# All adjacency loads on SyncE's queue instead of two queues, and half of the x loads of the prologue on GpSimd's

## The reference

```python
h = jnp.maximum(_layernorm(x), 0.0)                     # x: 4096 x 256 f32
mask = (adj > 0)
agg = mask @ h / jnp.maximum(mask.sum(1), 1.0)
combined = concat([h @ W_self + b_self, agg @ W_nb + b_nb])
x = x + relu(combined @ W_comb + b_comb)
h = jnp.maximum(_layernorm(x), 0.0)
Wh = (h @ W).reshape(n, 4, 64)
sl, sr = einsum(Wh, a_l), einsum(Wh, a_r)
e = leaky_relu(sl[:, :, None] + sr.T[None], 0.2)
alpha = softmax(where(adj | eye, e, -inf), axis=2)
x = x + elu(einsum('nhm,mhd->nhd', alpha, Wh))
```

## Time and profile before

| | |
|---|---|
| median of 3 runs | 863.46 us (859.91 to 865.07) |
| the profiled execution | 861.41 us, its span 859.6 us |
| PE busy | 796.0 us, 93% |
| DVE busy | 697.7 us, 81% |
| ACT busy | 562.6 us, 65% (issuing DMAs isn't counted) |
| POOL busy | 176.4 us, 21% |
| HBM read, written | 98.17 MB, 16.85 MB |
| ACT's queue (q10), SP's queue (q1), POOL's queue (q0) | 37.89 MB, 56.32 MB, 20.86 MB |

### The profile page before, as it was taken

One profiled execution on the slowest core, in us unless ns is written; L12 is line 12 of the kernel. 1 busy time (PEld: TensorE's weight loads), 2 busy tenths in 40 slices (PEclk: granted clock), 3 DMA queues, 4 the chain that ended last, 5 costly groups with the idle time before them and its releaser, 6 DMA issues.

```text
span 859.6 us, 26116 instructions
## 1 busy us (share of the span) xinstructions
PE 796.0 (93%) x10791; PEld 728.7 (85%) x10791; DVE 697.7 (81%) x1339; ACT 562.6 (65%) x840; POOL 176.4 (21%) x254
## 2 busy tenths in 40 slices
PE   5787769999999999879999999999999999999995
PEld 4333558888888888678999999999999999999995
DVE  3777747777777777587888999889999889998884
ACT  3464112222222222489999998999989999989992
POOL 0311136577667666200000000000000000000000
PEclk9999989999999999979999999999999999999998
DMA  6599999999999999230052012401201410111001
GB/s 153 151 270 262 302 293 306 312 296 336 298 264 288 276 281 250 86 84 26 0 98 49 14 35 49 92 17 38 49 12 37 98 49 12 37 49 49 9 16 37
DMA packets 90084, 115.68 MB, mean 135 GB/s; under 512 B 61580, under 2 KB 63440, under 8 KB 90032
## 3 DMA queue, kind: packets, MB, share of 16 engines
q1 hardware_dynamic: 67680, 56.32, 25.2%
q10 hardware_dynamic: 12384, 37.89, 15.9%
q0 software_dynamic: 9968, 20.86, 8.0%
HBM read 98.17 MB, written 16.85 MB: 134 GB/s over the span
## 4 chain that ended last, share of the span: by engine, by line
PE 61%; DVE 18%; ACT 9%; issue 6%; ACTq 4%; DMA 2%; DVEq 0%
PE ps_t L573 12%; PE ps_t L575 12%; PE ps_x L635 8%; PE ps_t L635 8%; PE ps_a L635 8%; ACT stage L770 5%; DVE stage L1067 4%; ACTq L333 4%; PE ps_w L635 4%; PE ps_h L635 4%; PE ps_w L594 2%; DVE stage L1057 2%; DVE stage L1078 2%; DVE g L1093 2%; PE ps_a L542 1%
## 5 line engine op out<-in xcount | busy, mean ns | idle before, releaser
L573 PE MATMUL ps_t<-g,mask 128*128 128x257 f16 x1024 | 231.1, 275 | 3.0 <-DVE mask L965 2.9
L575 PE MATMUL ps_t<-g,mask 128*128 128x256 f16 x1024 | 231.0, 274 | 0.0
L770 ACT ACTIVATE stage<-rows,sr 128x1024 int8<-128x1024 f32 x192 | 204.3, 1169 | 5.7 <-PE ps_w L635 5.7
L770 ACT ACTIVATE stage<-bits,sr 128x1024 int8<-128x1024 f32 x192 | 204.2, 1168 | 2.5 <-PE ps_w L635 2.5
L1067 DVE SCALAR_TENSOR_TENSOR stage<-stage,mask 128x1024 int32<-128x1024 int32 x128 | 156.1, 1220 | 21.8 <-ACT stage L770 21.1
L635 PE MATMUL ps_x<-g,stage 128*128 128x130 f16 x2048 | 158.8, 220 | 9.9 <-DVE stage L1078 4.7
L635 PE MATMUL ps_t<-g,stage 128*128 128x130 f16 x2048 | 158.6, 219 | 0.0
L635 PE MATMUL ps_a<-g,stage 128*128 128x130 f16 x2048 | 158.5, 219 | 0.0
L635 PEld LDWEIGHTS ps_x<-g,stage 128*128 128x128 fp8e4 x2048 | 127.4, 97 | 12.0 <-issue 11.9
L635 PEld LDWEIGHTS ps_a<-g,stage 128*128 128x128 fp8e4 x2048 | 127.4, 97 | 0.2
L635 PEld LDWEIGHTS ps_t<-g,stage 128*128 128x128 fp8e4 x2048 | 127.2, 97 | 0.2
(11 more groups left out here) (135 smaller groups left out, 826.5 us busy)
## 6 DMA issues: line engine op xcount, KB each, us to landing
mask<-in_adj ACTq DMA_DIRECT2D x84, 256.0 KB, 12.3
mask<-in_adj SPq DMA_DIRECT2D x68, 256.0 KB, 11.2
stage<-in_adj ACTq DMA_DIRECT2D x58, 256.0 KB, 9.2
stage<-in_adj SPq DMA_DIRECT2D x46, 256.0 KB, 8.6
own_scratch<-mask POOLq DMA_DIRECT2D x16, 256.0 KB, 5.0
rows<-own_scratch POOLq DMA_DIRECT2D x32, 128.0 KB, 6.7
rows<-in_x POOLq DMA_DIRECT2D x128, 32.0 KB, 7.2
x_scratch<-late POOLq DMA_DIRECT2D x32, 128.0 KB, 8.9
```

The lines of the kernel that those rows point to most:

```text
L573: nc.tensor.matmul(ps_t32[e][:, 0:D + 1], at, g[:, 2 * kk + b, D:2 * D + 1], start=kk + b == 0, stop=kk == NK - 1 and b == 1, skip_group_c ...
L575: last = nc.tensor.matmul(ps_t32[e][:, 0:D], at, g[:, 2 * kk + b, 0:D], start=False, stop=kk == NK - 1 and b == 1, skip_group_check=True)
L770: nc.scalar.activation(sign_bytes(sgn, k, b), srow[gr % 2].rearrange("p (r n) -> p r n", n=2 * P), ACT.Sign, bias=sr[:, 2 * k + b, H + gr ...
```

## The change

ACT issues no adjacency any more. SP issues all four quarters of every piece, in the order 0, 2, 1, 3: piece 0 behind the loads of x pairs 2 and 3; pieces 1 to 6 in halves, one half behind each x pair from 4 to 15; the rest behind those. Of each x pair from 4 on SP issues two transfers (0, 2) and POOL the other two (1, 3), on a semaphore of their own, `x_half_in`, for which `variances` waits too. The table `issued_at` goes.

```diff
-        def x_rows(eng, k):
+        def x_rows(eng, k, parts, landed):
-            for a in range(UN):
-                eng.dma_start(xin[k % XR][a * UP:(a + 1) * UP, :], x_v[a, k]).then_inc(x_in[k % XR], 16)
+            for a in parts:
+                eng.dma_start(xin[k % XR][a * UP:(a + 1) * UP, :], x_v[a, k]).then_inc(landed[k % XR], 16)
...
-            x_rows(sp, 2)
-            x_rows(sp, 3)
+            x_rows(sp, 2, (0, 2, 1, 3), x_in)
+            x_rows(sp, 3, (0, 2, 1, 3), x_in)
+            adj_rows(sp, 0, (0, 2, 1, 3))
             for k in range(XR, NK):
                 sp.wait_ge(h_ready, k - XR + 1)
-                x_rows(sp, k)
-            for n in range(BOTH, 2 * NT):
-                adj_rows(sp, n, range(UN // 2))
+                x_rows(sp, k, (0, 2), x_in)
+                adj_rows(sp, k // 2 - 1, (1, 3) if k % 2 else (0, 2))
+            for n in range(NK // 2 - 1, 2 * NT):
+                adj_rows(sp, n, (0, 2, 1, 3))
...
+            def x_half(k):
+                pool.wait_ge(h_ready, k - XR + 1)
+                x_rows(pool, k, (1, 3), x_half_in)
+
+            x_half(XR)
+            x_half(XR + 1)
             for k in range(NK):
                 store_own(k)
+                if k + XR + 2 < NK:
+                    x_half(k + XR + 2)
                 if k == 2:
                     row(0)
                     row(1)
...
                 high_hT(k, k % 2)
-                if k % 2 == 0:
-                    adj_rows(act, k // 2 - 1, (0, 2, 1, 3))
             highs(NK - 2, 0)
             highs(NK - 1, 1)
-            for n in range(BOTH, EARLY + 8):
-                adj_rows(act, n, range(UN // 2, UN))
-
...
                 norm1(t, t % 2)
-                for n in issued_at(2 * t):
-                    adj_rows(act, n, range(UN // 2, UN))
                 high_h1T(t, t % 2)
-                for n in issued_at(2 * t + 1):
-                    adj_rows(act, n, range(UN // 2, UN))
                 copy_wh(t, t % 2, t // 2)
...
             def variances(k):
-                dve.wait_ge(x_in[k % XR], (k // XR + 1) * 16 * UN)
+                if k < XR:
+                    dve.wait_ge(x_in[k], 16 * UN)
+                else:
+                    dve.wait_ge(x_in[k % XR], 16 * UN + k // XR * 16 * (UN // 2))
+                    dve.wait_ge(x_half_in[k % XR], k // XR * 16 * (UN // 2))
```

More of the change, by code:

```diff
@@ L212, in build @@
         x_in = [sem(f"x_in{i}") for i in range(XR)]
+        x_half_in = [sem(f"x_half_in{i}") for i in range(XR)]
         dve_step = sem("dve_step")
@@ L668, in _ @@
         def _(act):
-            x_rows(act, 0)
-            x_rows(act, 1)
+            x_rows(act, 0, range(UN), x_in)
+            x_rows(act, 1, range(UN), x_in)
             act.wait_ge(consts, 4)
@@ L1293 @@
 EARLY = 10
-BOTH = NK // 2 - 1
 def raw_slots():
@@ L1313 @@
 SLOT, LAST_IN = raw_slots()
[L1316 to L1324, removed]
 def reads_early(gr):
```

## The result

| | before | after |
|---|---|---|
| median | 862.9 us (859.91 to 865.07) | 847.78 us (845.19 to 849.03) |
| profiled execution, span | 859.6 us | 845.7 us |
| ratio of the times | | 0.9829, 95% interval 0.9808 to 0.9849 |

The change makes the kernel 1.7% faster, 15 us by the medians, 13.9 by the spans. Forecast were 843 us, in a range of 838 to 853.

The account below looks back on a forecast made before the run. The prediction took ACT's DMA issues to be on the path in the prologue and at the start of stage 1, otherwise PE's. Gains of 21.6 us less 0.5 and 2.9 gave 18.2, from 861.41 to 843 us, range 838 to 853.

Parts of the forecast that it names:

- ACT's issues in the prologue: Prologue: ACT's issues behind the even pairs 2 to 14 go, seven at 1.71 us each, 12.0 us won.
- The idle time ahead of the first W product: Start of stage 1: PE's idle time of 6.79 us before the first W product goes, 6.8 us won.
- The slow restart: First to second W product: the step falls from 10.37 to 7.92 us without the clock drop, 2.4 us won.
- Two steps of stage 1: Stage 1, 152.60 to 168.88 us: two tiles take 16.28 us instead of 15.84 through ACT's issues, 0.4 us won.
- POOL's burst: Prologue: x and ten row transfers behind the third store delay the fourth; 0.5 us lost, bounds 0 and 5.8.
- The DMA engines: Prologue: shorter pairs load the DMA engines more, `outputs` may wait for stores; 2.9 us lost, between nothing and 5.8.
- One queue can carry it: SP's adjacency issues: 1.41 us each reflects crowding on shared engines; one queue reaches what three did, sum unchanged.
- the third rival: Stage 1: SP's queue is the limit, at 1.41 us a transfer 903 us; decides above 0.99 us a transfer; chance 0.05.
- The first rival: Prologue: stores landing after 8.6 us bound the pairs, the 12.0 us gain is gone; 852 to 861 us; chance 0.14.
- The second: Stage 1 begins no earlier in step: the first W product waits for another engine, say DVE; 849 us; chance 0.08.
- The fourth: Prologue: POOL is held up, each issue taking 1.29 us beside DVE work; 4.9 us more, 848 us; chance 0.03.

Follow-up runs that it names:

- e1_rows_late: The changed kernel with row(0) moved behind the store of pair 10 and row(1) behind that of pair 11; 0.9758 of the kernel before, median 842.9 us.

## Why the prediction was right, and where it was wrong

The sign, the range and what the change takes away hold; 847.8 is 5 us above the forecast. The prologue, forecast at 12.0 - 0.5 - 2.9 = 8.6 us, gave 4.2, and the rest, forecast at 9.6, gave 9.8. That the total came so near is in part luck: one debit was 6.3 us too small, another 2.9 us too large. By its steps:

1. *ACT's issues in the prologue, 12.0 us.* Right. Between the transposes there are 3.46 us in every pair that no wait touches, but for one pair (5.19 us, before as after) in which DVE also turns the first piece; six of the seven issues fall between pairs 3 and 15, 10.3 us, and with 6.8 lost to the store 3.5 remain, where 3.3 are measured (53.5 us before, 50.2 after). Without that loss, in e1_rows_late, the first sum of stage 1 starts at 84.20, 10.9 us sooner than before.
2. *The idle time ahead of the first W product, 6.8 us.* Right: 7.4 (11.6 less 4.2).
3. *The slow restart, 2.4 us.* Right: 2.3.
4. *Two steps of stage 1, 0.4 us.* Won and lost again. At the end of stage 1 a piece comes late:

```profile
328.13 1.23 DVE L964 TENSOR_SCALAR bits<-stage 128x2048 uint8<-128x2048 int32 x1 [0.40 <-DMA stage<-in_adj]
```

5. *POOL's burst, "I take 0.5 us".* **This is the step that failed.** It named the store and the burst, and measured is 6.8 us. Three terms of its sum were too kind. The store was 3.15 us late, not 2.5: the 6.0 us left out the third store's own issue, 0.57. It took 7.6 us to land, not 5.0: I took the median of all stores for one that stands behind ten row transfers and two of x in its own queue; with the rows away it took 5.5. And its buffer was wanted after 5.6 us, not 6.92: 6.92 runs from the start of one `outputs` to the start of the one after the next, but the store can go out only when the first has written its last part. 3.15 + 7.6 - 5.6 is the measured 5.17 us within rounding, below the upper bound of 5.8 (7.1 with the right cover). The bound left out what the idle time does to PE's clock, 1.6 us more, although step 3 had just priced the same thing elsewhere. e1_rows_late gives the 6.8 back.
6. *The DMA engines, 2.9 us.* Too high. In the free pairs 303 GB/s are wanted at 3.46 us, and pairs stay at 3.46; the lower bound, nothing, was right. The reason given there, that the adjacency may fall behind, was hardly needed: e1_rows_late moved 291, 297 and 305 GB/s from 40 to 68 us, so the 266 GB/s of the kernel before were no limit. The late waits for stores (0.24, 0.95, 0.41 us) are no longer than before.
7. *One queue can carry it.* True for the changed kernel, and the 1.41 us an issue on which the doubt and the third rival stood was misread. Of the 19.78 us of the earlier trace rows SP spent 10.0 waiting for the semaphore of a slot, that `norm` is done with all pairs:

```profile
SPq L333 <- ACT mask L683: 10.0, 1, 10.0
```

The 14 issues themselves took 9.8 us, 0.70 each. Issues of 2 us and more are there in the same trace on ACT alone, up to 3.2 us each among those from 108.4 to 118.3, whose transfers take 31.8 us and more to land. The prediction also costed the order 0, 2, 1, 3 not at all, and there the doubt was justified: with 0, 1, 2, 3 W products are 9.6 and 9.7 us apart at the end of stage 1 (323.58, 333.18, 342.91, in the execution of 881.3 us), some 1.2 us a transfer against the limit of 0.99 that the rival named, and nothing is left of the gain. The rule of the Trainium skill that the prediction cites, on issuing engines, is not contradicted; it isn't enough.

The first rival, stores landing late throughout, did not come: one store did. The second did not. The fourth: one store takes 1.30 us to issue, as before, and the x transfers beside other DVE work take 1.00 for two.

Sum by the trace: 4.2 + 7.4 + 2.3 + 0.1 = 14.0 us by the last W product, 13.9 in the span.

## What to carry to other kernels

An engine's DMA issues are work in its order: where the engine feeds a chain, move them to one that doesn't, and count on the receiving engine what stands in front of each store whose buffer is waited for, at the landing time of a queue with that much in it. Price a wait of TensorE with the slow clock that follows it. Where loads are split by partitions, try an order in which consecutive transfers of one queue go to different halves of SBUF, before counting queues. Count the cover of a buffer from the end of the step that fills it to the start of the one that wants it, not from start to start; and take the waits for semaphores out of a row of issues before dividing by their number.

Of the kernels here, the changed one with the ten row transfers moved behind the stores of pairs 10 and 11 beats both: 0.9758 of the kernel before, and 0.974 with x on SP alone.

## What was not expected of the hardware

- The order of transfers of 32 partitions in one queue was worth 1.9 and 2.6% of the kernel's time. From 118 to 240 us the order 0, 2, 1, 3 moved 308 to 318 GB/s in four executions of 840.7 to 847.7 us and 291 and 285 in two of 860.0 and 855.8; the order 0, 1, 2, 3 moved 266 and 261, in executions of 881.3 and 887.1 us. The DMA share was 1.03 or 1.04 in all of them: that share does not tell how much is moved.
- A store of 256 KB on POOL's queue landed after 5.5 us, after 7.0 behind five row transfers and after 6.7, 7.2 and 7.6 behind ten, at the same place in the prologue.
- Behind 5.25 us of idle time of PE, which ended at 53.97, the granted clock was 0.60 in the five microseconds from 50 on and 0.71 in the next five, and the same six matmuls took 2.74 us instead of 1.47.
- Once stage 1 is PE's throughout, it lives on a lead of adjacency: the changed kernel waited 0.40 us for data, the one that starts it 6.7 us sooner 2.8 us.
